# One row-maximum instruction for two heads, over two neighbouring PSUM banks, with the even head's score block moved to the end of its slot

## What is computed

```python
h = _sln(hidden, w, ln_g, ln_b, Wg, bg, Wb, bb)
qkv = (h @ Wqkv.T + bqkv).reshape(B, N, num_heads, hd, 3)
q = jnp.moveaxis(qkv[..., 0], 2, 1)
k = jnp.moveaxis(qkv[..., 1], 2, 1)
v = jnp.moveaxis(qkv[..., 2], 2, 1)
energy = jnp.einsum('bhqd,bhkd->bhqk', q, k)
att = jax.nn.softmax(energy, axis=-1) / D ** 0.5
out = jnp.einsum('bhqk,bhkd->bhqd', att, v)
out = jnp.moveaxis(out, 1, 2).reshape(B, N, D)
out = out @ Wp.T + bp
h1 = out + hidden
h2 = _sln(h1, w, ln_g, ln_b, Wg, bg, Wb, bb)
return h2 + h1
```

## Time and profile before

| | |
|---|---|
| median of three runs | 363.55 us (361.94 to 365.43) |
| profiled execution | 363.79 us |
| its span in the trace | 361.9 us |
| PE busy | 339.1 us (94%) |
| DVE busy | 301.7 us (83%) |
| ACT busy | 249.3 us (69%) |
| GpSimd busy | 161.8 us (45%) |
| row maxima (line 572), DVE | 256 instructions, 172.9 us |
| granted TensorE clock, mean | 0.971 |

### The profile page before, as it was taken

The page is one execution under the profiler, slowest core; times in us unless marked ns, Lnnn a source line. Parts: engine busy times, 40 slices in busy tenths (PEclk is TensorE's granted clock), DMA queues, the critical chain, the costliest instruction groups (busy, mean ns, idle before and its releaser), DMA issues.

```text
span 361.9 us, 8937 instructions
## 1 busy us (share of the span) xinstructions
PE 339.1 (94%) x3161; PEld 291.3 (80%) x3161; DVE 301.7 (83%) x729; ACT 249.3 (69%) x487; POOL 161.8 (45%) x203
## 2 busy tenths in 40 slices
PE   8697999999999999999999999999999999998960
PEld 4566878888898988888888989888888888886640
DVE  4678977789898989889898989898998989895463
ACT  5534586868687786868686868768686866667720
POOL 5615361526454644627173545455371723243222
PEclk9869999999999999999999999999999999999985
DMA  8195345444454544555535544444554544500000
GB/s 242 64 221 154 115 120 147 122 131 119 126 146 132 132 127 131 144 149 148 149 102 156 133 130 131 129 130 132 147 147 120 147 122 111 142 19 31 31 29 29
DMA packets 45257, 44.68 MB, mean 123 GB/s; under 512 B 6015, under 2 KB 40846, under 8 KB 45214
## 3 DMA queue, kind: packets, MB, share of 16 engines
q1 hardware_dynamic: 41470, 42.02, 42.1%
q10 hardware_dynamic: 1696, 1.57, 1.8%
q0 software_dynamic: 2048, 0.53, 0.9%
HBM read 5.79 MB, written 4.19 MB: 28 GB/s over the span
## 4 chain that ended last, share of the span: by engine, by line
PE 86%; DVE 3%; ACT 3%; DMA 3%; issue 2%; POOL 0%; POOLq 0%; SPq 0%; DVEq 0%; ACTq 0%
PE m L787 25%; PE pv L787 18%; PE st L787 18%; PE sa L787 16%; PE pv L873 4%; PE pv L947 2%; DMA wqkv<-WqkvT_dram 2%; PE m L913 2%; ACT p L511 1%; DVE mx L572 1%; DMA qst<-m_l 1%; DVE qk_l L607 1%; ACT oT L461 1%; PE pv L887 1%; PE m L887 0%
## 5 line engine op out<-in xcount | busy, mean ns | idle before, releaser
L572 DVE TENSOR_REDUCE mx<-sa 128x2 f32<-128x512 f32 x256 | 172.9, 686 | 30.2 <-PE sa L787 27.8
L511 ACT ACTIVATE p<-st 128x512 f32<-128x512 f32 x256 | 150.2, 598 | 40.4 <-PE st L787 35.7
L787 PE MATMUL st<-qst,kst 128*128 128x256 f32 x512 | 108.3, 294 | 2.0 <-ACT p L511 1.0
L787 PE MATMUL sa<-kst,qst 126*128 126x256 f32 x512 | 105.5, 288 | 2.5 <-DVE mx L572 2.2
L787 PEld LDWEIGHTS st<-qst,kst 128*128 128x128 f32 x512 | 78.1, 189 | 17.2 <-issue 13.0
L787 PEld LDWEIGHTS sa<-kst,qst 126*128 126x128 f32 x512 | 79.2, 191 | 4.8 <-DVE mx L572 4.4
L322 POOL DMA_DIRECT2D qst<-m_h x32 | 18.2, 567 | 117.5 <-DVE m_l L581 117.5
L787 PE MATMUL pv<-p,v_st 128*32 128x256 f32 x1024 | 61.9, 382 | 0.3 <-ACT p L511 0.3
L787 PEld LDWEIGHTS pv<-p,v_st 128*32 128x32 f32 x1024 | 30.0, 109 | 21.8 <-ACT p L511 2.4
L363 POOL TENSOR_TENSOR rstd<-vare,minus_half 128x4 f32<-128x4 f32 (+1 forms) x19 | 17.2, 905 | 55.8 <-DVE vare L629 36.5
L787 PE MATMUL m<-hT_h,wqkv_h 128*128 128x256 f32 x128 | 38.4, 308 | 2.2 <-DVE hT_l L651 2.2
(11 more groups left out here) (104 smaller groups left out, 556.1 us busy)
## 6 DMA issues: line engine op xcount, KB each, us to landing
qst<-qk_h SPq DMA_DIRECT2D x64, 128.0 KB, 2.4
qst<-qk_l SPq DMA_DIRECT2D x64, 128.0 KB, 2.5
kst<-qk_h SPq DMA_DIRECT2D x60, 128.0 KB, 2.5
kst<-qk_l SPq DMA_DIRECT2D x60, 128.0 KB, 2.8
xa<-x_dram SPq DMA_DIRECT2D x16, 256.0 KB, 3.0
out_dram<-y SPq DMA_DIRECT2D x16, 256.0 KB, 2.2
wqkv<-WqkvT_dram SPq DMA_DIRECT2D x1, 512.0 KB, 6.5
kst<-qk_h ACTq DMA_DIRECT2D x4, 128.0 KB, 4.4
```

The source lines that it names most:

```text
L511: nc.scalar.activation(p32[:, h, :], st_ps[h % 2][:], ACT.Exp).then_inc(exp_done, 1)
L572: dve.tensor_reduce(mx[:, par(a), h // HH, (h % HH) * TT:(h % HH + 1) * TT], sa_ps[h % 2][:].rearrange("p (t n) -> p t n", t=TT), AX.X, AL ...
L787: return nc.tensor.matmul(o, l, r, start=start, stop=stop)
```

## The change

The two banks of `sa` become one tensor of two neighbouring banks. DVE takes the maxima of heads h - 1 and h with one instruction when the odd block is there (256 instructions of 512 elements per partition become 128 of 1024). `max_done` is raised by two per pair, and a score block of either head waits until the whole pair before is taken. On PE the odd head's block stays where it was, right behind `scores`; the even head's moves behind all other matmuls of its slot.

```diff
-        sa_ps = [pb("sa0"), pb("sa1")]
+        sa_pair = ctx.enter_context(nc.psum_tensor("sa", [P, 2, 512], F32))
+        sa_ps = [sa_pair[:, 0, :], sa_pair[:, 1, :]]
...
             def maximum(a, h):
                 if not has(a):
                     return
+                if h % 2 == 0:
+                    return
                 wait(dve, sa_done, 16 * a + h + 1)
                 wait(dve, mT_done, 2 * (a - 2) + h // HH + 1)
-                if first(a) and h == 0:
+                if first(a) and h == 1:
                     dve.wait_ge(mx_zero, 1)
-                dve.tensor_reduce(mx[:, par(a), h // HH, (h % HH) * TT:(h % HH + 1) * TT],
-                                  sa_ps[h % 2][:].rearrange("p (t n) -> p t n", t=TT),
-                                  AX.X, ALU.max).then_inc(max_done, 1)
+                dve.tensor_reduce(mx[:, par(a), h // HH, (h % HH - 1) * TT:(h % HH + 1) * TT],
+                                  sa_pair[:].rearrange("p h (t n) -> p (h t) n", t=TT),
+                                  AX.X, ALU.max).then_inc(max_done, 2)
...
-                wait(pe, max_done, 16 * a + h - 1)
+                wait(pe, max_done, 16 * a + h - h % 2)
...
                     if has(b):
                         scores(b, h)
-                    scores_max(b + 1, h)
+                    if h % 2:
+                        scores_max(b + 1, h)
...
                         project_qk(1, 1, m1, k_done, h)
+                    if h % 2 == 0:
+                        scores_max(b + 1, h)
```

## The result

| | before | changed |
|---|---|---|
| median | 362.93 us (4 runs) | 407.71 us (404.82 to 408.94, 4 runs) |
| ratio, 95% interval | | 1.121 (1.113 to 1.130) |
| span of the profiled execution | 361.9 us | 406.8 us |

The sign and the mechanism were as forecast. The size was not: 387.5 us was given, with a range up to 398, and the loss is 45 us instead of 24.

A forecast was written before the change was run, and what follows sets the result against it. PE's full queue was taken as the bound. Pauses 14.0 + 7.8, less 4.2 given back, plus start 3.8 and step 0 2.4, made +23.8 us, so 387.5 us; range 377 to 398.

The forecast's parts named there:

- The wait from odd to even block, 1.69 us: Odd block's start to next even block's: 0.44 us to the reduction's start, 1.21 for the reduction, 0.04 for the semaphore.
- The three pauses: PE idle per mid-run step: 0.95 us before head 12's block, 0.05 before head 14's, 0.60 before the next step's head 0.
- The covered windows: Pairs 0,1 to 8,9 of each step: PE's other work was to fill the 1.69 us wait, costing nothing.
- Given back: Time saved in slot 10 and at slot 2's `weigh`: 0.3 us per step, between 0 and 0.6.
- Steps 1 to 14: Steps given the same pauses before heads 12 and 14: 14 x (0.95 + 0.05) = 14.0 us.
- The start, +3.8 (2 to 5): Step -1, where PE has little else: a pair cycles in 2.03 us, delaying slot 1 of step 0 by 3.8 us.
- step 0, +2.4: No output projection, so its last three windows are uncovered: 6.57 us from head 11's block to slot 1, against 4.15.
- the fourth rival: Pauses halve PE's granted clock in slots 12 to 15: 60 us on top, about 447 us; chance 2%.
- D: Length of the long reduction over two banks: taken as 1.21 us, bounds 0.69 and 1.37.
- DVE sets the pace: Rival: DVE is late everywhere, each pair saves about 0.09 us, so about 352 us; chance 3%.
- the waits are absorbed: Rival: PE's pauses fall where it would have waited anyway, so 362 to 364 us; chance 3%.
- D is nearer to two instructions: Rival: the long reduction takes 1.37 us, more windows fall short, so 397 to 401 us; chance 8%.

The follow-up runs named there:

- f_covered_pairs: g_own_start with heads 0 to 9 of samples 1 to 15 reduced in pairs by the long instruction, all others singly; 371.96 us, ratio 1.024.
- a_order_only: Kernel before with only the even score blocks moved to the end of their slots, one reduction per head at its old place; 404.03 us, ratio 1.110.
- g_own_start: Changed kernel's PE order, one reduction per head directly ahead of the odd head's, each awaiting its own block and releasing its own bank; 366.38 us, ratio 1.008.
- c_two_together: Changed kernel with two 512-element reductions in place of the long one, both behind the odd block, banks released together; 407.26 us, ratio 1.120.
- e_busy_fill: Changed kernel plus matmuls on zeros in the waits for maxima of steps -1 and 0; 404.95 us, ratio 1.116.
- i_busy_fill_again: e_busy_fill run once more, beside the unaltered changed kernel on the same chip; 404.91 us, ratio 1.113, against that kernel's 406.10 us.

## Why the prediction was right in kind and wrong in size

The rule was right: a pause is the time that the pair's hand-over and reduction need, less PE's work in between. What failed is the sum that was made with it. It took five windows of every step as covered at no cost, credited 0.3 us per step that is not there, treated steps 0 and 14 like the others where they have less work, and made step -1 too short. Of the 21.1 us that are missing 9.0 lie in the eleven mid-run steps, 6.9 up to slot 10 of step 1, 4.5 in the last steps and 0.8 at the end.

- **What bounds the kernel**: right. DVE's 8.6 us less of busy time (13 had been forecast), and f_covered_pairs with 75 instructions fewer, gained nothing. That doesn't make DVE's program indifferent: in a_order_only DVE is busy for 73% of the span, and the order of its instructions costs 38 us (404.03 us against g_own_start's 366.38).
- **The wait from odd to even block, 1.69 us**: measured 1.78. The duration was right within 0.02. The reduction's start was mis-sized: I took 0.44 us from the short reductions, the long one needs 0.51. Before head 0 it is 1.88, as 0.14 us instead of 0.04 pass from the reduction's end to the block (also in c_two_together); that block waits for a second semaphore as well, and I haven't tested whether it is that.
- **The three pauses, 0.95 + 0.05 + 0.60 = 1.60 per step**: found in these three places. The step of 21.87 us less the 19.95 of f_covered_pairs, which has none of them, is 1.92, so they were mis-sized by 0.32.
- **The covered windows, taken at nothing**: 0.20 us per step by f_covered_pairs against g_own_start. Here the prediction called the cover thin and still took zero.
- **Given back, 0.3 per step**: wrong, it is nothing. g_own_start has the changed PE order with no pair and stands at 19.75, as before. I had read the gaps at 165.57 and before `weigh` as time to be saved; in the new order gaps of like size stand at other places.
- These make 1.92 + 0.20 = 2.12 in place of 1.30, which over eleven steps is 9.0 of the 21.1 us that were missing.
- **"Steps 1 to 14" treated alike**: wrong, and a slip in reading the code. Step 14 has no q and k projections, since there is no sample 16. The changed kernel's timeline there:

```profile
355.62 0.50 PE L790 MATMUL sa<-kst,qst 126*128 126x256 f32 x2
...
357.98 0.50 PE L790 MATMUL sa<-kst,qst 126*128 126x256 f32 x2 [0.90 <-DVE mx L575]
...
360.33 0.50 PE L790 MATMUL sa<-kst,qst 126*128 126x256 f32 x2 [0.70 <-DVE mx L575]
```

These are the even blocks of heads 2, 4 and 6. Those of heads 4 and 6 pause, 0.90 and 0.70 us, where the mid-run step has a covered window. From step 12 to 16 the loss is 7.75 us instead of 3.3. Step 0 is such a case too: its slot 2 has no `weigh`, as there is no sample -1, and the changed kernel's block of head 2 waits 0.65 us there (at 49.85), in a window that had been called covered.
- **The start, +3.8 (2 to 5), and step 0, +2.4**: 9.15 + 3.90 = 13.05 together. Of it 0.9 is there ahead of anything the change touches (the q projection begins at 23.46 instead of 22.58 us); two executions of one kernel can differ by as much (22.44 in e_busy_fill, 23.54 in i_busy_fill_again). The first `sa` block, behind the first quarter now, costs 0.7, the stretch from it to slot 1 of step 0 costs 6.0 (20.44 us against 14.47), and from there to slot 10 it is 1.6 (10.81 against 9.23), which the sum did not have at all. PE's timeline in step -1:

```profile
31.52 0.74 PE L790 MATMUL sa<-kst,qst 126*128 126x256 f32 x4 [1.03 <-DVE mx L575]
33.66 0.74 PE L790 MATMUL sa<-kst,qst 126*128 126x256 f32 x4 [1.39 <-DVE mx L575]
...
41.55 1.21 PE L790 MATMUL sa<-kst,qst 126*128 126x256 f32 x4 [1.39 <-DVE mx L575]
44.15 1.22 PE L790 MATMUL sa<-kst,qst 126*128 126x256 f32 x4 [1.39 <-DVE mx L575]
```

A pair cycles in 2.14 us (2.03 was taken), and in 2.60 at the lower clock. That is the fourth rival on a small scale: it had been put in the short windows of every step and weighed 2%, but came in steps -1 and 0, where PE has the least to do, and cost 2.3 to 2.4 us. From 70 us to the last steps the clock stays at 1.00 in spite of the pauses. The row quoted against it was of the kernel before and did not carry over: from 30 to 40 us the changed kernel's PE is busy for 6.54 us and granted 0.83, from 40 to 50 us for 6.16 and granted 0.66. The rule of the Trainium skill on cycling through the PSUM queue ("TensorE: Matmul & The Clock Gate") held at the start, by these rows, and not in mid-run, where the clock granted from 70 to 390 us is 1.00.
- **The range**: every term erred in the same direction, and its upper end was set mostly by a longer D, which was the term I knew best.
- The rivals "DVE sets the pace" and "the waits are absorbed" are excluded by the time itself (407.7 us, where they gave 352 and 362 to 364), the first also by c_two_together, which has the 128 instructions back and the same time. "D is nearer to two instructions" is excluded by the 1225 ns.

## What to carry to other kernels

Two banks filled in turn and drained by one instruction are one buffer: the producer waits for hand-over, drain and hand-over less the work it has in between, at every place where that work is shorter. Go through all such windows, the first and last steps too, where a pipeline has less to fill them with. When a producer's work is moved later, move the consumer's instruction in its own program as well; left in place it blocks everything behind it (404 us against 366 us here, by DVE's order alone). Merging instructions on an engine that isn't the bound gave nothing back here.

## What the hardware showed that was not expected

- A reduction of 1024 PSUM elements over two banks takes 1225 ns against 2 x 686, and starts 0.10 us behind the end that the trace gives the matmuls (193.69 to 193.79), two of 512 in the same place 0.04 us (191.06 to 191.10). What the merging saves in length it gives back at the start.
- TensorE's granted clock fell to 0.66 between 40 and 50 us, when PE was busy for 6.2 of 10 us, and stayed at 1.00 in mid-run with three pauses in each step, up to 0.78 us without work on PE.
